# A graph layer with attention, a mixing branch and experts: the skip rows are loaded and added in the last stage instead of in the mixing branch

## The reference

```
xn = layernorm(x)
# graph branch: 8 heads of 32
q, k, v = xn Wq + bq, xn Wk + bk, xn Wv + bv;   e = edge_attr We
alpha = sum over the head of q[dst] * (k[src] + e) / sqrt(32)
w = softmax of alpha over the edges of one dst
gnn = segment_sum((v[src] + e) * w, dst) + (xn Wskip + bskip)
# mixing branch: linear attention over all nodes, then feed-forward
y = layernorm(xn + attend(xn) Wo + bo) * g1 + b1
mix = layernorm(y + relu(y W1 + b1) W2 + b2) * g2 + b2
x = x + gnn + mix
# last stage: 8 experts, each three products, weighed by a router
h = layernorm(x)
out = x + sum over e of w_e * (relu(bn(relu(bn(h W1e)) W2e)) Woe + bo_e)
```

## Time and profile before

| | us |
|---|---|
| median of 3 timed runs | 3518.64 (3511.38 to 3543.4) |
| the profiled execution | 3552.69, span 3550.9 |
| PE, PEld busy | 3186.8 (90%), 2479.1 (70%) |
| DVE busy | 2793.7 (79%) |
| ACT, POOL busy | 1682.8 (47%), 1646.0 (46%) |
| DMA | 593.53 MB, 167 GB/s over the span |

### The profile page before, as it was taken

How to read it: one execution, slowest core, us unless ns; L and a number is a source line. 1 busy time by engine, 2 the same in 40 slices (tenths; PEclk the granted TensorE clock), 3 DMA queues, 4 the chain that set the end, 5 groups by cost and what they waited for, 6 DMA issues and landing times.

```text
span 3550.9 us, 72164 instructions
## 1 busy us (share of the span) xinstructions
PE 3186.8 (90%) x17312; PEld 2479.1 (70%) x17312; DVE 2793.7 (79%) x5687; ACT 1682.8 (47%) x4460; POOL 1646.0 (46%) x1803
## 2 busy tenths in 40 slices
PE   4997999999999999999999188888769999999999
PEld 3776666666666666666666155555569999999998
DVE  6775888888888888888887889999846666666665
ACT  1222333333333343333333256666546777777776
POOL 1223777777777777777775077777600000000000
PEclk9998899999999999999999599999979999999999
DMA  7345999899989899999998267777600000000000
GB/s 178 116 119 156 251 256 254 248 254 261 257 247 253 248 264 261 260 256 255 266 255 223 92 200 231 232 230 231 194 4 19 12 13 16 12 17 12 13 15 9
DMA packets 520909, 593.53 MB, mean 167 GB/s; under 512 B 187937, under 2 KB 396979, under 8 KB 520319
## 3 DMA queue, kind: packets, MB, share of 16 engines
q1 hardware_dynamic: 312408, 351.02, 34.0%
q0 software_dynamic: 201888, 232.77, 25.1%
q10 hardware_dynamic: 6409, 7.46, 0.7%
HBM read 426.91 MB, written 163.17 MB: 166 GB/s over the span
## 4 chain that ended last, share of the span: by engine, by line
PE 62%; DVE 12%; issue 8%; DMA 7%; SPq 3%; DVEq 3%; another core or an unknown queue 2%; ACT 1%; POOL 1%; ACTq 0%; POOLq 0%
PE psum L684 10%; PE psum L686 10%; PE psum L685 10%; PE psum L903 8%; PE psum L762 7%; PE psum L746 7%; PE psum L826 3%; DMA weights<-kv_tab,idx 3%; PE psum L817 2%; DVEq L1616 2%; DVE weights L1427 2%; DVE region_s L1613 1%; DVE part L1441 1%; DMA ve_d<-weights 1%
## 5 line engine op out<-in xcount | busy, mean ns | idle before, releaser
L625 POOL DMA_INDIRECT weights<-kv_tab,idx x450 | 549.1, 1220 | 254.5 <-issue 150.1
L762 PE MATMUL psum<-region_x,weights 125*125 x1800 | 493.3, 397 | 72.8 <-issue 39.7
L1183 ACT ACTIVATE region_s<-psum,bns 128x250 f32<-128x250 f32 x800 | 402.9, 554 | 287.8 <-PE psum L686 287.8
L746 PE MATMUL psum<-we,weights 64*125 64x256 f32 x1800 | 525.4, 410 | 0.0
L1665 DVE TENSOR_TENSOR parts_h<-region_s,parts_h 128x500 fp32r<-128x500 f32 x400 | 269.8, 679 | 311.2 <-ACT parts_h L1187 283.7
L903 PE MATMUL psum<-region_s 125*125 125x264 f32 x1800 | 452.5, 401 | 68.0 <-DVE region_s L1613 68.0
L1066 ACT ACTIVATE weights<-psum,region_s 125x250 f32<-125x250 f32 x450 | 211.3, 470 | 609.8 <-PE psum L754 289.0
L903 PEld LDWEIGHTS psum<-region_s 125*125 125x125 f32 x1800 | 304.6, 188 | 215.7 <-issue 76.9
L762 PEld LDWEIGHTS psum<-region_x,weights 125*125 125x125 f32 x1800 | 325.2, 191 | 177.3 <-issue 136.0
L625 POOL DMA_INDIRECT kv_more<-kv_tab,idx x300 | 370.4, 1235 | 126.9 <-issue 84.7
L746 PEld LDWEIGHTS psum<-we,weights 64*125 64x125 f32 x1800 | 298.5, 186 | 183.0 <-issue 155.2
(11 more groups left out here) (247 smaller groups left out, 7515.0 us busy)
## 6 DMA issues: line engine op xcount, KB each, us to landing
region_s<-ve_d SPq DMA_DIRECT2D x450, 256.0 KB, 3.0
ve_d<-weights SPq DMA_DIRECT2D x225, 256.0 KB
ve_d<-kv_more SPq DMA_DIRECT2D x150, 256.0 KB
weights<-in_attr_t SPq DMA_DIRECT2D x450, 62.5 KB
ve_d<-region_r SPq DMA_DIRECT2D x75, 256.0 KB
kv_tab<-region_s SPq DMA_DIRECT2D x50, 224.0 KB
region_s<-ab_d SPq DMA_DIRECT2D x450, 1.0 KB
weights<-kv_tab,idx POOLq DMA_INDIRECT x450
```

The source lines that it names most:

```text
L625: nc.gpsimd.indirect_dma_start(kg[r][0:T, w, :], None, kv_tab, bass.IndirectOffsetOnAxis(idx[:, r, w:w + 1], 0)).then_inc(gathered[r], 16)
L746: last = mm(psum[0:T, s % 2, w * D:(w + 1) * D], att_b[:, s % RP, w * T:(w + 1) * T], we[:, :], start=True, stop=True)
L762: last = mm(psum[0:T, 2 + s % 2, w * D:(w + 1) * D], hott[:, s % RA, w * T:(w + 1) * T], q_all[:, bass.ds(j, 1), :].rearrange("p o d -> p ...
L1183: last = fn(fh[:, layer, o, :], psum[:, bk + e % 2, o * BN:(o + 1) * BN], ACT.Relu, bias=bns[:, layer, 1, col:col + 1], scale=bns[:, layer ...
```

## The change

- SP no longer loads skip rows in the score pass: `load_skip` and its calls are gone, and with them the semaphore `m_res_in`.
- add2 is gone from DVE's table. gain2 writes `mout` itself and counts `m_outr`. The buffer `mres` keeps its place and isn't used.
- In the last stage `load_res` issues a second DMA, skip_d into `fx2`, after the one of res_d. For blocks from 2 on it first waits for `f_bo` of the block that had the buffer before. Both loads count on `f_in`, and the residual waits for both.
- The residual adds twice: fres to the skip rows in `fx2`, then the sums to that.

```diff
-            def load_skip(b):
-                wait(sp, m_outr, b)
-                for cut in CUTS:
-                    sp.dma_start(mres[cut, :, :], skip_d[bass.ds(b * BN, BN), :].rearrange("(t p) d -> p t d", p=T)[cut]).then_inc(m_res_in, 16)
-
...
-                    if s == 1 and not (isinstance(b, int) and b < 2):
-                        load_skip(b - 2)
...
-            load_skip(NB - 2)
...
                 store_mix(sp, NB - 2)
-                load_skip(NB - 1)
                 store_mix(sp, NB - 1)
...
                 sp.dma_start(fres[:, u], res_d[bass.ds(b * BN, BN), :].rearrange("(t p) d -> p t d", p=T)).then_inc(f_in[u], 16)
+                if not (isinstance(b, int) and b < 2):
+                    sp.wait_ge(f_bo, b - 1)
+                sp.dma_start(fx2[:, u], skip_d[bass.ds(b * BN, BN), :].rearrange("(t p) d -> p t d", p=T)).then_inc(f_in[u], 16)
...
                 elif g == "gain2":
-                    order(tt(mx2[:, :, :], mx2[:, :, :], row2(R_G2), ALU.mult))
-                elif g == "add2":
-                    dve.wait_ge(m_res_in, (b + 1) * 32)
-                    tt(mout[:, :, :], mx2[:, :, :], mres[:, :, :], ALU.add).then_inc(m_outr, 1)
+                    tt(mout[:, :, :], mx2[:, :, :], row2(R_G2), ALU.mult).then_inc(m_outr, 1)
...
-            last_at = {3: "norm2", 5: "gain2", 6: "add2"}
+            last_at = {3: "norm2", 5: "gain2"}
...
-                dve.wait_ge(f_in[u], (b // 2 + 1) * 16 if isinstance(b, int) else (b - u) * 8 + 16)
+                dve.wait_ge(f_in[u], (b // 2 + 1) * 32 if isinstance(b, int) else (b - u) * 16 + 32)
...
-                order(tt(fx2[:, u], fgn, fres[:, u], ALU.add))
+                order(tt(fx2[:, u], fx2[:, u], fres[:, u], ALU.add))
+                order(tt(fx2[:, u], fgn, fx2[:, u], ALU.add))
```

More of the change, by code:

```diff
@@ L223, in build @@
         mxt = carve(0, 2, 2, BN)
-        mres = carve(None, 2, D, parts=T)
+        carve(None, 2, D, parts=T)
         mq, mqe, mqp = (carve(None, 2, BN) for _ in range(3))
@@ L303, in build @@
         m_var, m_root = sem("m_var"), sem("m_root")
-        m_stored, m_y_read, m_res_in = sem("m_stored"), sem("m_y_read"), sem("m_res_in")
+        m_stored, m_y_read = sem("m_stored"), sem("m_y_read")
         gather_go = sem("gather_go")
```

## The result

Over 20 executions each, the changed kernel takes 3542.6 us (median; 3529.31 to 3560.97) and the kernel before 3529.78 (3511.38 to 3546.07). The ratio is 1.0036, with a 95% interval of 1.0019 to 1.0053: the change costs about 12.8 us. That is within 1%, but the sign is not the forecast one, and 3542.6 lies outside the range of 3487 to 3536. Of the 28.6 us between forecast and result, 11 come from the base: the three times shown had a median of 3518.64, the twenty have 3529.78. The other 17.5 are an error of the sum, -4.7 against +12.8.

A forecast was written before the change was run, and what follows sets the result against it. It took the score pass as bound by a chain over several engines, the last stage by TensorE. Terms -7 -3 -0.6 +2.1 +1.5 +2.3 = -4.7 us against 3552.69, carried to the 3518.64 median, gave 3514 us, range 3487 to 3536.

The forecast's parts named there:

- What bounds the kernel: Score pass: no engine full, the chain of waits runs over several; last stage: TensorE busy for all of 800 us.
- SyncE's issues and VectorE's add, -7: Score pass: removing skip-load issues (7.3 us on the chain) and adds (3.6 us) gives back about two thirds, -7 us.
- Rival 1: Score pass: nothing comes back there; total +5.3 us, 3524 us; chance 0.22.
- Traffic, -3: Score pass: 6.1 MB less, 1.5% of its bytes, shortens the landings on the chain by 3 us.
- Rival 2: Score pass goes by its bytes: -25 us there, -30.6 in all, 3488 us; chance 0.17.
- VectorE as the bound: Score pass, within the bytes rival's case: 25 adds at 0.69 us would give -17 us.
- The change-over, -0.6: Between score pass and sums: the add in VectorE's tail, on the chain, goes, -0.6 us.
- First load, +2.1: Last stage, block 0: the residual also waits for the uncovered skip load, 256,000 bytes more, +2.1 us.
- Two adds on the chain, +1.5: Last stage, blocks 0 and 1: the chain runs over the residual, so two extra VectorE adds cost +1.5 us.
- Steady, +2.3: Last stage, 23 later blocks: the add's 0.73 us delay about uses up the slack, 0.1 us each, +2.3 us.
- Rival 3: Last stage: the add stalls TensorE at layer2, up to 0.73 us a block, +16.8; total +9.8, 3528 us; chance 0.12.
- The base: Whole kernel: terms summed against the profiled execution's 3552.69 us, then carried to the three timed runs' median, 3518.64 us.

The follow-up runs named there:

- gone with filling: Kernel before without skip loads and adds anywhere, plus 27 idle instructions in VectorE's program ahead of its wait for the ids: ratio 0.9990, -3.5 us.
- gone: Kernel before with skip loads and adds removed from the score pass and not put in the last stage: ratio 1.0023, +8.1 us.
- after: The changed kernel itself, against the kernel before: 3542.6 us, ratio 1.0036.
- after with filling: Changed kernel plus 54 long satisfied waits (27 instructions) in VectorE's program ahead of its wait for the ids: ratio 1.0023 to the kernel before, +8.1 us.

## Why the prediction was wrong

*What bounds the kernel* was read rightly for the last stage and wrongly for the pass. There I took the chain's pieces on SyncE and VectorE for time that comes back in part. I wrote that the next path is close, and then kept two thirds all the same.

*SyncE's issues and VectorE's add, -7: the step that failed first.* The ten pieces on L466 and six on L1496 are where the chain happened to run. The add's time in the earlier trace rows and the issues' in the earlier trace rows were right as durations, but not as prices. The pass over all kernels without the loads and adds, with the repeating terms taken off the timed difference: gone with filling -3.3 (interval 4.2 either way), gone +0.8 (6.2), after +0.5 (6.0), after with filling +2.8 (7.4). Weighed by their intervals that is -0.8, with about 3 to either side (two of the four share their executions of the kernel before, so it is rather more). -10 is excluded, by the first of the four alone; -7 with nothing for the traffic is beyond the weighed value, but just inside the first one's own interval. Rival 1 was right for the pass. The reason is in part argued. For SyncE the queue has free time behind one pair in the same step, step 1 is hardly longer with two (3.51 us), and the cost does not grow evenly with the pairs; but the term by itself, 4.9 for one pair, is excluded neither by the loads left out nor by the second pair. For VectorE it is seen in one profile (the next steps catch up), and the timed runs don't settle it.

*Traffic, -3.* No run resolves 3 us. The loads left out gave -5.7 with -13.4 to +2.5. Adding bytes costs (59 us for three copies that are both read and written), removing 1.5% did not show. Rival 2, a pass that goes by its bytes (-25), is excluded. So is its other form, VectorE as the bound. The rule of the Trainium skill ("Perfetto Trace Analysis", section "Identifying the Most-Contended Engine") had put VectorE or DMA ahead of TensorE in the pass. For VectorE the runs don't agree with it as a guide to the price: no adds, or four times as many, left the pass where it was within their intervals. For DMA they leave it open.

*The change-over, -0.6:* -0.72. *First load, +2.1:* the landing 6.48 - 4.39 = 2.1, and 2.5 from the last multiply to the residual. The Trainium skill's rule on the split ("DMA: Bandwidth & Descriptors", section "Why a DMA increments its semaphore by 16 and not by 1") agrees with the trace: the split load landed 1.26 us earlier, and I had written 1.0. *Two adds on the chain, +1.5:* about +1.0. *Steady, +2.3:* +2.0, at the place named (layer2's first weight load 0.11 us late). Rival 3, the stall of 0.73 in each block, did not come; the slack of 0.67 to 0.78 counted nearly in full.

*What was missing altogether: +7.5 us in the sums' loop.* The prediction walked the stages that the diff touches and said nothing of the one between. No row of the prediction shows the slow place, though the trace of the kernel before has it, in the loop's second step. Still, the change makes VectorE's instruction stream shorter ahead of a loop, and I didn't ask what moves with it.

*The base.* I summed against an execution that was itself long (3552.69, pass 1581 us where later ones had 1569) and carried the sum to a median of three. With twenty, it was 11 us higher.

By terms: -4.7 forecast, +9.2 for the pass (-0.8 instead of -10), +7.5 for the loop, and -0.5 for the rest make +11.5, against 12.8 measured with 6 to either side.

## What to carry to other kernels

A piece of the chain is a price only if nothing beside it has free time. Before taking work away, ask how long its queue stands idle in the same step, and test it by adding more of the same: here four pairs cost 42 us and two cost nothing that could be measured, so the price of four said nothing of what the first would give back. Taking instructions out of one place moves every later loop of that engine in its instruction stream. After such a change compare the stages that were not touched first, and try some idle instructions as filling before judging the change.

## What the hardware showed

VectorE's queue takes 0.096 us longer (0.225 instead of 0.129) at one place in its instruction stream, on every iteration of a loop of 49 instructions that lies over it. The place did not move when the loop did, and the next one was 256 instructions further on. At the loop's end it cost 7.5 us over 75 iterations, 0.1 each, more than in the second step. There it still cost 5 us against a loop clear of it, although I had taken it for hidden. The two together are 12 to 14 us, 0.17 an iteration, which is more than the 0.096 of the place itself; what makes up the rest, no run shows. The Trainium skill ("Runtime: NRT & Kernel Launch", section "Instruction fetch mechanics") says that instructions are refilled in blocks of 256 and that crossing a boundary is "mostly hidden". The spacing agrees; hidden it was in none of the loops that lay over the place. That the block boundary is the cause is inferred from the spacing, not shown by a record.

A pair of DMA issues holds SyncE's queue for 1.31 us, six of 1 KB for 3.91 and six of full size (in the kernel with four full pairs) for 4.93, each a median over the blocks, so it is mostly their number that holds it and not their bytes. The same add of 125 by 512 floats takes 0.69 us on VectorE and 1.29 on GpSimd, and TensorE's granted clock over the pass was 0.96 and 0.95 in the two kernels with four pairs, whose steps are longer, and 0.98 before.
